# A selective scan shared by VectorE, GpSimd and ScalarE: all of y's sums on GpSimd, the saved last columns on ScalarE

## What is computed

```python
def step(h, xs):
    d_t, B_t, C_t, u_t = xs
    dA = jnp.exp(d_t[..., None] * A)
    h = h * dA + (d_t * u_t)[..., None] * B_t[:, None, :]
    y_t = jnp.einsum('bdn,bn->bd', h, C_t)
    return (h, y_t)
...
y = jnp.moveaxis(ys, 0, 1) + u * D_param
y = y * jax.nn.silu(gate)
```

## Time and profile before

| | |
|---|---|
| runs of the kernel before, median (lowest to highest) | 4261.53 us (4258.79 to 4261.58) |
| profiled execution, span from first to last instruction | 4258.0 us |
| its mean granted TensorE clock, share of full speed | 0.895 |
| busy: PE, DVE, ACT, POOL | 79%, 89%, 52%, 63% |

### The profile page before, as it was taken

How to read it: one execution, slowest core, us unless ns; L and a number is a source line. 1 busy time by engine, 2 the same in 40 slices (tenths; PEclk the granted TensorE clock), 3 DMA queues, 4 the chain that set the end, 5 groups by cost and what they waited for, 6 DMA issues and landing times.

```text
span 4258.0 us, 51800 instructions
## 1 busy us (share of the span) xinstructions
PE 3374.2 (79%) x12672; PEld 2422.9 (57%) x12672; DVE 3807.6 (89%) x6958; ACT 2216.3 (52%) x3820; POOL 2672.4 (63%) x1991
## 2 busy tenths in 40 slices
PE   5555555557989989889898898998988989887547
PEld 4444444435666666666666566665666666655334
DVE  8999999935989898998989898989899898989892
ACT  2332333314756656566666575665656666655550
POOL 3454555522958576675859595858667585957470
PEclk8777777778999999999999999999999999998778
DMA  2111111120111111111111111111111111101110
GB/s 90 50 50 50 45 50 50 37 99 23 33 32 35 35 45 23 43 29 44 29 37 37 32 38 31 35 35 45 23 43 28 45 28 38 37 30 27 27 37 5
DMA packets 119088, 164.72 MB, mean 39 GB/s; under 512 B 8512, under 2 KB 75712, under 8 KB 118336
## 3 DMA queue, kind: packets, MB, share of 16 engines
q1 hardware_dynamic: 118848, 162.54, 13.5%
HBM read 128.29 MB, written 25.69 MB: 36 GB/s over the span
## 4 chain that ended last, share of the span: by engine, by line
DVE 29%; issue 20%; PE 11%; POOL 8%; ACT 7%; DVEq 2%; POOLq 0%; ACTq 0%; SPq 0%; DMA 0%
DVE D L1115 15%; PE W L875 6%; POOL dBu L731 5%; DVE prod L1133 4%; POOL yacc L744 3%; DVE hc L1122 2%; ACT D L838 2%; PE W L925 1%; PE W L952 1%; PE W L948 1%; DVE yacc L1145 1%; ACT L838 1%; ACT yacc L813 1%; DVE D L1136 1%; ACT dBu L823 1%
## 5 line engine op out<-in xcount | busy, mean ns | idle before, releaser
L1115 DVE TENSOR_TENSOR_SCAN D<-D,hc,dBu 128x256 f32<-128x256 f32 x2048 | 1525.5, 746 | 0.0
L731 POOL TENSOR_TENSOR dBu<-U,BC 128x512 f32<-128x512 f32 x1024 | 1314.2, 1293 | 312.3 <-DVE U L1104 280.9
L875 PE MATMUL W<-nT,wffn 128*128 128x256 f32 x5632 | 1295.0, 394 | 200.9 <-ACT nT L770 198.9
L875 PEld LDWEIGHTS W<-nT,wffn 128*128 128x128 f32 x5632 | 1102.1, 196 | 396.6 <-ACT nT L770 215.4
L838 ACT ACTIVATE D<-delta,A 128x256 f32<-128x256 f32 x2048 | 868.6, 465 | 878.6 <-DVE yacc L1145 636.1
L744 POOL TENSOR_TENSOR yacc<-yacc,prod 128x512 f32<-128x512 f32 x736 | 937.5, 1274 | 335.6 <-DVE prod L1133 331.5
L907 PE MATMUL W<-wffn,hT 128*128 128x512 f32 (+1 forms) x1408 | 630.3, 604 | 36.1 <-DVE hT L1033 36.1
L875 PE MATMUL W<-nT,win 128*128 128x256 f32 x2048 | 477.3, 396 | 62.5 <-ACT nT L770 62.5
L1133 DVE TENSOR_TENSOR prod<-D,BC 128x512 f32<-128x512 f32 x736 | 495.4, 673 | 0.0
L875 PEld LDWEIGHTS W<-nT,win 128*128 128x128 f32 x2048 | 408.0, 200 | 141.9 <-ACT nT L770 73.7
L907 PEld LDWEIGHTS W<-wffn,hT 128*128 128x128 f32 (+1 forms) x1408 | 269.0, 195 | 364.5 <-issue 315.4
(11 more groups left out here) (119 smaller groups left out, 3923.6 us busy)
## 6 DMA issues: line engine op xcount, KB each, us to landing
BC<-bc_scratch SPq DMA_DIRECT2D x256, 256.0 KB, 4.6
XM<-x_scratch SPq DMA_DIRECT2D x29, 512.0 KB, 4.9
X<-x_scratch SPq DMA_DIRECT2D x17, 512.0 KB, 3.7
ix<-idx SPq DMA_DIRECT2D x32, 260.0 KB, 3.4
wffn<-nA SPq DMA_DIRECT2D x32, 260.0 KB, 2.3
X<-x SPq DMA_DIRECT2D x16, 512.0 KB, 3.8
XR<-x SPq DMA_DIRECT2D x16, 512.0 KB, 3.8
x_scratch<-XR SPq DMA_DIRECT2D x16, 512.0 KB, 3.0
```

What stands on the lines that cost most here:

```text
L731: nc.gpsimd.tensor_tensor(dBu[e % 4][:], U[:, 2 * j:2 * j + 2, :], BC[slot][:, 0:1, :].to_broadcast([P, 2, CH]), ALU.mult).then_inc(s_dBu, 1)
L875: last = T_.matmul(dst, lhsT, rhs, start=(n == 0), stop=(n == len(terms) - 1))
L1115: V.tensor_tensor_scan(D[:, m, :], D[:, m, :], dBu[e % 4][:, m % 2, :], hc[:, n, m:m + 1], ALU.mult, ALU.add).then_inc(s_scan, 1)
```

## The change

All four pairs of a state index now go through `prod` and are added by POOL, in every step; DVE's own adds (L1145) and its product in place (L1136) are gone, and with them `pool_pairs`, `steps_less`, `pool_sums`, `dve_sums` and the semaphore `s_hC`. The save of the last column is now ACT's, an Identity activation with scale `kp`; it stands ahead of the exps that write over the same part of `D`, and these wait for it. `kp` is a one-column buffer into which DVE copies the step's `keep` at the start of the step. DVE issues both scans of pair e and then the product of e - 1.

```diff
--- before.py
+++ after.py
@@ -536,6 +536,7 @@
         xext = [buf(ctx, f"xext{s}", [2, CH + KC - 1]) for s in range(2)]
         cc = buf(ctx, "cc", [ME, KC - 1])
         hc = buf(ctx, "hc", [S, ME])
+        kp = buf(ctx, "kp", [1])
         BC = [buf(ctx, f"BC{s}", [2, CH]) for s in range(3)]
         dBu = [buf(ctx, f"dBu{s}", [2, CH]) for s in range(4)]
         prod = [buf(ctx, f"prod{s}", [2, CH]) for s in range(2)]
@@ -555,7 +556,7 @@
         m_dt, m_dtl, m_dp, m_abs, m_relu = sem("m_dt"), sem("m_dtl"), sem("m_dp"), sem("m_abs"), sem("m_relu")
         m_exp, m_ln, m_delta, m_du = sem("m_exp"), sem("m_ln"), sem("m_delta"), sem("m_du")
         s_dA, s_dBu, s_scan, s_hc = sem("s_dA"), sem("s_dBu"), sem("s_scan"), sem("s_hc")
-        s_prod, s_hC, s_acc = sem("s_prod"), sem("s_hC"), sem("s_acc")
+        s_prod, s_acc, m_kp = sem("s_prod"), sem("s_acc"), sem("m_kp")
         m_y, m_out, m_res = sem("m_y"), sem("m_out"), sem("m_res")
 
 
@@ -610,21 +611,6 @@
         def side_late(f1):
             return 1 - SIDE_EARLY if f1 else SIDE_EARLY
 
-
-        def pool_pairs(f1):
-            return 3 if f1 else 2
-
-        def steps_less(i):
-
-            return max(i - (NC - 2), 0) if isinstance(i, int) else 0
-
-        def pool_sums(i):
-
-            return S * (3 * i - steps_less(i))
-
-        def dve_sums(i):
-
-            return S * (i + steps_less(i))
 
         def rows(p):
 
@@ -734,22 +720,20 @@
                     def add(e):
 
                         n, j = divmod(e, 4)
-                        r = pool_pairs(f1) * n + j
                         pool.wait_ge(s_prod, NE * i + e + 1)
-                        if r == 0:
+                        if e == 0:
                             pool.wait_ge(m_skip, ME * (i + 1))
                         if n:
-                            pool.wait_ge(s_acc, pool_sums(i) + r - pool_pairs(f1) + 1)
+                            pool.wait_ge(s_acc, NE * i + e - 3)
                         y = yacc[:, 2 * j:2 * j + 2, :]
-                        nc.gpsimd.tensor_tensor(y, y, prod[r % 2][:], ALU.add).then_inc(s_acc, 1)
+                        nc.gpsimd.tensor_tensor(y, y, prod[e % 2][:], ALU.add).then_inc(s_acc, 1)
 
                     for e in range(4):
                         outer(e)
                     for e in range(NE):
                         if e + 4 < NE:
                             outer(e + 4)
-                        if e % 4 < pool_pairs(f1):
-                            add(e)
+                        add(e)
                         if e == F2_STAT:
                             root(norm_no(*late(i)))
                         if more and e == at["m_stat"]:
@@ -827,11 +811,20 @@
                         if k >= 2:
                             act.wait_ge(m_exp, 4 * i + k - 1)
                             N_.activation(dBu[k - 2][:], dBu[k - 2][:], ACT.Ln, bias=1.0).then_inc(m_ln, 1)
+                    def save(e):
+
+                        n, j = divmod(e, 4)
+                        act.wait_ge(s_prod, NE * i + e + 1)
+                        N_.activation(hc[:, n, 2 * j:2 * j + 2], D[:, 2 * j:2 * j + 2, CH - 1], ACT.Identity,
+                                      scale=kp[:]).then_inc(s_hc, 1)
+
+                    act.wait_ge(m_kp, i + 1)
                     for e in range(NE):
 
                         n, j = divmod(e, 4)
                         if e >= 4:
-                            act.wait_ge(s_prod, NE * i + e - 3)
+                            save(e - 4)
+                            act.wait_ge(s_hc, NE * i + e - 3)
                         else:
                             act.wait_ge(m_delta, 4 * i + e + 1)
                         for m in (2 * j, 2 * j + 1):
@@ -853,6 +846,8 @@
                                 silu(ffn_no(*late(i)), norm_no(*late(i)), p, side_late(f1))
                         if more and e == min(at["m_evac"], NE - 1):
                             evac(norm_no("M", i + 1), 1 - side_late(f1))
+                    for e in range(NE - 4, NE):
+                        save(e)
 
                 act.wait_ge(small_loaded, 80)
                 N_.activation(A[:], A[:], ACT.Exp).then_inc(b_setup, 1)
@@ -952,7 +947,7 @@
                             bc = T_.matmul(W[0][0:2 * S, 2, :], wx[:, k, R:R + 2 * S], U[:, k, :], start=(k == 0), stop=(k == ME - 1))
                     bc.then_inc(m_bc, 1)
 
-                    pe.wait_ge(s_prod, NE * i)
+                    pe.wait_ge(s_hc, NE * i)
                     pe.wait_ge(m_dtl, i + 1)
                     for m in range(ME):
                         last = chain(D[:, m, :], [(wdt[:, m * P:(m + 1) * P], dtl[:])])
@@ -1041,8 +1036,7 @@
 
                 def gate_y(i):
 
-                    dve.wait_ge(s_acc, pool_sums(i + 1))
-                    dve.wait_ge(s_prod, NE * (i + 1))
+                    dve.wait_ge(s_acc, NE * (i + 1))
                     dve.wait_ge(m_sg, 2 * (i + 1))
                     for h in range(2):
                         g = sgm[:, 4 * h:4 * h + 4, :]
@@ -1075,6 +1069,9 @@
 
                 def step(i, back, f1, more):
                     at = places(f1)
+
+                    dve.wait_ge(s_hc, NE * i)
+                    V.tensor_copy(kp[:], keep[:, bass.ds(i + 1, 1)]).then_inc(m_kp, 1)
                     for q in range(ME // 2):
                         conv(i, q)
                     if f1:
@@ -1115,45 +1112,20 @@
                         V.tensor_tensor_scan(D[:, m, :], D[:, m, :], dBu[e % 4][:, m % 2, :], hc[:, n, m:m + 1],
                                              ALU.mult, ALU.add).then_inc(s_scan, 1)
 
-                    def save(e):
+                    def times_c(e):
 
                         n, j = divmod(e, 4)
+                        dve.wait_ge(bc_loaded[n % 3], 16 * ((6 if n % 3 == 0 else 5) * i + n // 3 + 1))
+                        dve.wait_ge(s_acc, NE * i + max(e - 1, 0))
                         dve.wait_ge(s_scan, 2 * NE * i + 2 * e + 2)
-                        V.tensor_scalar(hc[:, n, 2 * j:2 * j + 2], D[:, 2 * j:2 * j + 2, CH - 1], keep[:, bass.ds(i + 1, 1)], None,
-                                        ALU.mult).then_inc(s_hc, 1)
-
-                    def times_c(e):
-
-                        n, j = divmod(e, 4)
-                        h_, r = D[:, 2 * j:2 * j + 2, :], pool_pairs(f1) * n + j
-                        c_ = BC[n % 3][:, 1:2, :].to_broadcast([P, 2, CH])
-                        dve.wait_ge(bc_loaded[n % 3], 16 * ((6 if n % 3 == 0 else 5) * i + n // 3 + 1))
-                        if j < pool_pairs(f1):
-                            dve.wait_ge(s_acc, pool_sums(i) + max(r - 1, 0))
-                            V.tensor_tensor(prod[r % 2][:], h_, c_, ALU.mult).then_inc(s_prod, 1)
-                        else:
-                            dve.wait_ge(s_hc, NE * i + e + 1)
-                            V.tensor_tensor(h_, h_, c_, ALU.mult).then_inc(s_hC, 1)
-
-                    def add(e):
-
-                        n, j = divmod(e, 4)
-                        pair, mine = slice(2 * j, 2 * j + 2), 4 - pool_pairs(f1)
-                        dve.wait_ge(m_skip, ME * (i + 1))
-                        dve.wait_ge(s_prod, NE * i + e - 3)
-                        dve.wait_ge(s_hC, dve_sums(i) + mine * n + j - pool_pairs(f1) + 1)
-                        V.tensor_tensor(yacc[:, pair, :], D[:, pair, :], yacc[:, pair, :], ALU.add).then_inc(s_prod, 1)
+                        V.tensor_tensor(prod[e % 2][:], D[:, 2 * j:2 * j + 2, :], BC[n % 3][:, 1:2, :].to_broadcast([P, 2, CH]),
+                                        ALU.mult).then_inc(s_prod, 1)
 
                     for e in range(NE + 4):
                         j = e % 4
                         if e < NE:
                             scan(e, 2 * j)
-                        if 1 <= e <= NE:
-                            save(e - 1)
-                        if e < NE:
                             scan(e, 2 * j + 1)
-                        if 2 <= e <= NE + 1 and (e - 2) % 4 >= pool_pairs(f1):
-                            add(e - 2)
                         if 1 <= e <= NE:
                             times_c(e - 1)
                         if e == NE + 1:
```

More of the change, by code:

```diff
@@ L1116, in scan @@
                                              ALU.mult, ALU.add).then_inc(s_scan, 1)
-                    def save(e):
-                        n, j = divmod(e, 4)
-                        dve.wait_ge(s_scan, 2 * NE * i + 2 * e + 2)
-                        V.tensor_scalar(hc[:, n, 2 * j:2 * j + 2], D[:, 2 * j:2 * j + 2, CH - 1], keep[:, bass.ds(i + 1, 1)], None,
-                                        ALU.mult).then_inc(s_hc, 1)
                     def times_c(e):
                         n, j = divmod(e, 4)
-                        h_, r = D[:, 2 * j:2 * j + 2, :], pool_pairs(f1) * n + j
-                        c_ = BC[n % 3][:, 1:2, :].to_broadcast([P, 2, CH])
                         dve.wait_ge(bc_loaded[n % 3], 16 * ((6 if n % 3 == 0 else 5) * i + n // 3 + 1))
```

(17 more changed lines are left out.)

## The result

The changed kernel takes 4363.4 us (median of 4, 4360.2 to 4366.2) against 4260.2 us (4258.6 to 4261.6) of the kernel before on the same chip: a ratio of 1.0243, with a 95% interval of 1.0228 to 1.0257. It is 103 us slower. The forecast was slower by 46 us (4307.5), with a range of 4278 to 4350. The direction and the engine that binds were right, more than half of the loss was missing, and the time lies outside the range.

A forecast was written before the change was run, and what follows sets the result against it. The prediction took DVE as full now and POOL as the bound after the change: 45 us over the step boundaries plus 1.0 in steps 14 and 15, on 4258.0, plus 3.5 for the median, gave 4307.5 us, range 4278 to 4350.

The forecast's parts named there:

- What binds: Steps 0 to 13: POOL becomes the bound, 157 us a step before any wait, where DVE needs 140.
- signs named: DVE busy down by some 280 us; POOL idle for DVE products only at pairs 2 and 57; others besides.
- Start: From a step's first scan: add(0) starts after 3.4 us, outer(7) at 10.95.
- Middle: outer(7) to the end of add(54): 104 POOL operations, 127.7 us, +0.4 for the norm at pair 27.
- End: After add(54): DVE's norm at pair 57 waits for POOL's root; gate_y starts at 159.9, 3.35 us later than before.
- Does the next step notice?: Step boundaries: gate_y's delay passes in full at 12 back edges, 3.5 us each; two others 1.5 each; 45 us.
- Steps 14 and 15: Scan phases of these steps, without early FFN: 160.7 us (-1.3) and 159.1 (+2.3), together +1.0.
- ACT: 64 saves a step on ACT at 0.25 us each, range 0.1 to 0.5; ACT otherwise costed at nothing.
- Sum: Whole kernel: 45 + 1.0 = +46 us on the span of 4258.0, plus 3.5 for the median: 4307.5 us.
- (a): POOL binds but gate_y's delay is mostly hidden and only ACT's chain counts: +22, 4283.5 us; chance 17%.
- (b): ACT's saves and late table reloads make POOL wait, 2 to 6 us more per step: 4335 to 4400; chance 15%.
- (c): Faster: POOL is never kept waiting after its start, -17 us, 4244.5 us; chance 5%.

The follow-up runs named there:

- k2: The changed kernel with the saves on DVE again, only the sums on POOL: 4369.0 us, ratio 1.0252 to the kernel before.
- k10: k1 with the root for pair 57's norm issued right behind its variance, before outer(58), instead of after add(55): 4288.4 us, ratio 1.0061.
- k1: The changed kernel with POOL made to wait for norms at pairs 27 and 57 and the variance at pair 55 (step 14: own places): 4302.9 us.
- k11: The changed kernel with one pause alone: POOL waits before outer(58) until the variance of pair 55 is written; 4336.4 us, ratio 1.0173.
- k8: k6 with POOL also given three of four sums in steps 14 and 15: 4154.6 us, ratio 0.9743 to the kernel before.
- k3: The kernel before, sums unchanged, with ACT saving the columns of the pairs that POOL adds: 4199.4 us, ratio 0.9855.
- k6: k3 plus two pauses of POOL, before add(26) and add(56), until the norm is through: 4171.1 us, ratio 0.9782.

## Why the prediction was right and wrong

- **What binds.** Right: POOL at 16.00 of 16.00 us in the stretch above, DVE's saved time in its waits (k2 against the changed kernel). Two of the signs named did not show: DVE's busy time fell by 127 us and not by 280, and POOL idled for DVE at pairs 27 and 55 too.
- **Start.** Right: 3.42 and 11.04 us against 3.4 and 10.95.
- **Middle.** This is the step that failed. "The norm at pair 27 runs beside POOL, 2.41 us instead of some 1.0 alone", at +0.4 in all, took its price from a row in which POOL had stood idle three operations earlier. With a POOL that had run without pause since pair 2 the norm was shut out, and the price was 2.7 us of idle POOL. "The statistics (1.89) fit" looked at their compute alone: their last instruction, the variance, belongs to the same kind, and cost 2.0 us at pair 55. From outer(7) to the end of add(54) were 130.8 us for 128.05, and from there to gate_y 23.1 for 20.9. With the 0.1 of the start these are the 5.1 us between 159.9 and 165.0: 2.5 are the stall at pair 27 (2.9 from start to start, less the 0.4 forecast) and 2.0 that at pair 55.
- **End.** Right in kind, 1 us a step by k10. In the changed kernel itself DVE waits 0.23 us for the root, for 2.4 forecast, as the stall at pair 55 holds it first; in k1 it is 1.99.
- **Does the next step notice?** Partly wrong. "The delay passes in full" took the gap at the back edge as fixed, and it is shorter here, where DVE had been waiting just before: gate_y ends at 2228.52 and kp is copied at 2230.11, 1.59 us, where it was 2.80; over the 12 back edges the mean fell from 2.7 to 1.2. From the first scan of step 1 to that of step 13 a step grew by 7.5 us on average, while gate_y came 8.6 later in it.
- **Steps 14 and 15.** 162.8 and 158.8 against 160.7 and 159.1; step 14 has a variance of 3.55 us in the trace, with POOL idle for 1.99 us behind it, step 15 has none.
- **ACT.** Right: 0.256 us a save, and no scan waited for ACT.
- **Sum.** 89.9 over the loop's 12 back edges, 6.3 and 5.9 at the two boundaries outside the loop, 0.7 and 0.4 in the last two steps, less 1.6 in the first part of the program, make 101.6; the spans differ by 101.5. With the two instructions freed (k1) the time is 4302.9, beside the forecast of 4307.5. That closeness is in part luck: k1 pays 2.5 us a step in pauses, its gate_y comes at 160.9 instead of 159.9, and against that the sum passed the whole delay over the back edge, where in k1 a step grew by 3.2 us and gate_y by 4.3.
- **Rivals.** (a) had the wrong size, and not only ACT's chain counted: a step grew by 7.5 us where the evacuation moved by 6.7. (b) had the size, 4335 to 4400, but not the cause. (c) did not occur: also k10 stays 0.6% slower. The section of the Trainium skill's page "Perfetto Trace Analysis" that the prediction set beside (c) also says that GpSimd and VectorE share a read port, so that moving operations between those two might not help. The prediction left that half out; the 60 us that k1 wins back by keeping the two apart agree with it.

## What to carry to other kernels

Before work moves to an engine, ask how full that engine gets, and then what on the relieved engine needs a gap in it: a price taken while the neighbour had gaps does not hold once it has none. Where GpSimd runs back to back, VectorE's tensor_scalar from SBUF to SBUF, even a tiny one, should stand where GpSimd waits anyway, and a short wait put on purpose on the engine that binds can pay: in k11 0.19 us of it took away 1.99 us of idle time. A busy share can hold time in which an instruction only waits for a neighbour, so look at the length of one instruction too. Of a change with two halves, run each alone: here one was worth -62 us and the other more than +100.

## What the runs showed of the hardware that was not expected

- A DVE tensor_scalar from SBUF to SBUF, issued while POOL ran without pause and had two to four more operations ready, waited for all of them: 6.18 us for the norm (1.28 with POOL paused), 3.90 us for 128 x 2 (0.21). It was so at pair 27 of every step with an early FFN in the changed kernel, at pair 55 of the same steps, and at its like in step 14.
- It is not the moment within a POOL operation: the variance at pair 2 (the row at 2067.84) was issued while a POOL operation ran, and took 0.54 us. Nor does the number of ready operations settle it. The variance of step 14 met two behind the running one, an add and an outer, and waited through both:

```profile
3984.65 3.55 DVE L1012 TENSOR_SCALAR veps<-mv 128x2 f32<-128x2 f32 x1
...
3985.69 1.26 POOL L729 TENSOR_TENSOR yacc<-yacc,prod 128x512 f32<-128x512 f32 x1
...
3986.91 1.26 POOL L717 TENSOR_TENSOR dBu<-U,BC 128x512 f32<-128x512 f32 x1
```

The norm at pair 57 of step 5 met two as well, add(56) and outer(61), and got in at the next boundary with each half (1.40 and 1.48 us).

- What does part these rows in the changed kernel is how long POOL had run without idling: 47 operations or more (some 56 us), the running one counted, where an instruction was shut out, and at most 4 where one got in. No run varied this alone, and in k8 three of the variances at pair 55 waited one operation longer (2.0 instead of 0.8 us) after only 5. How the port is handed over stays open.
- The form with an accumulator is free of it: 0.80 us per half, POOL's spacing unchanged.
- DVE's gap at the back edge of the loop is not a constant. It was 2.1 to 3.1 us in the kernel before and 2.3 to 3.8 us in k3, k6 and k8, where DVE came to gate_y having waited under 0.4 us, and 0.8 to 1.6 us in the changed kernel, 0.7 to 1.8 us in k1 and k10, where it had waited 2.0 us for POOL's last add just before. No run shows why.
